# Scan layer of a four-layer stack: gate, SiLU, softplus steps and one spread of B moved within a task

## The reference

```python
xr = x @ in_w.T
u, res = (xr[..., :d_in], xr[..., d_in:])
...
u = _silu(jnp.transpose(uc + conv_b[None, :, None], (0, 2, 1)))
A = -jnp.exp(Alog)
xdbl = u @ xproj_w.T
delta = jax.nn.softplus(xdbl[..., :dt_rank] @ dt_w.T + dt_b)
Bm = xdbl[..., dt_rank:dt_rank + D_STATE]
Cm = xdbl[..., dt_rank + D_STATE:]
dA = jnp.exp(jnp.einsum('bld,dn->bldn', delta, A))
dBu = jnp.einsum('bld,bln,bld->bldn', delta, Bm, u)
...
    h = dA_t * h + dBu_t
    return (h, jnp.einsum('bdn,bn->bd', h, C_t))
...
y = jnp.moveaxis(ys, 0, 1) + u * D
y = y * _silu(res)
return y @ out_w.T
```

## Time and profile before

| | |
|---|---|
| median of 3 runs | 21318.11 us (21314.53 to 21318.33) |
| profiled execution, its own time | 21309.68 us |
| its span | 21307.9 us |
| VectorE (DVE) busy | 18447.0 us, 87% |
| GpSimd (POOL) busy | 17170.0 us, 81% |
| TensorE (PE) busy | 13655.5 us, 64% |
| ScalarE (ACT) busy | 11409.1 us, 54% |
| scan layer | from about 2250 to 18000 us |

### The profile page before, as it was taken

How to read it: one execution, slowest core, us unless ns; L and a number is a source line. 1 busy time by engine, 2 the same in 40 slices (tenths; PEclk the granted TensorE clock), 3 DMA queues, 4 the chain that set the end, 5 groups by cost and what they waited for, 6 DMA issues and landing times. The chain is left out here.

```text
span 21307.9 us, 183765 instructions
## 1 busy us (share of the span) xinstructions
PE 13655.5 (64%) x47074; PEld 4924.9 (23%) x47074; DVE 18447.0 (87%) x11898; ACT 11409.1 (54%) x12716; POOL 17170.0 (81%) x7352
## 2 busy tenths in 40 slices
PE   4875665665565565565565565565565668888885
PEld 2331111111111111111111111111111124444444
DVE  5778888888888888888888888888888878888886
ACT  1115555555555555555555555555555546666663
POOL 3768888888888888888888888888888868888881
PEclk8887777777777777777777777777777779999997
DMA  3225445545545545545445545545545521111113
GB/s 118 93 88 124 122 117 125 122 119 125 122 116 125 122 119 125 122 117 125 123 119 124 123 117 124 123 119 124 123 117 124 123 69 29 30 30 30 31 29 131
DMA packets 615483, 2240.63 MB, mean 105 GB/s; under 512 B 74881, under 2 KB 92147, under 8 KB 591091
## 3 DMA queue, kind: packets, MB, share of 16 engines
q1 hardware_dynamic: 610146, 2232.63, 41.6%
q10 hardware_dynamic: 5265, 7.14, 0.1%
HBM read 990.77 MB, written 174.96 MB: 55 GB/s over the span
## 5 line engine op out<-in xcount | busy, mean ns | idle before, releaser
L1357 POOL TENSOR_TENSOR h<-h,c_bc 128x1024 f32<-128x1024 f32 x4096 | 9593.6, 2356 | 1393.6 <-DVE h L1309 1393.1
L1309 DVE TENSOR_TENSOR_SCAN h<-da,state,px 128x1024 f32<-128x1024 f32 x3328 | 7810.8, 2347 | 444.7 <-DVE px L1303 165.2
L1174 ACT ACTIVATE da<-d_bc,a_neg 128x1024 f32<-128x1024 f32 x3328 | 3784.1, 1144 | 4012.1 <-DVE h L1309 3990.2
L1303 DVE TENSOR_TENSOR px<-px,du_bc 128x1024 f32<-128x1024 f32 x3328 | 4098.4, 1231 | 442.0 <-PE px L1002 221.2
L1016 PE MATMUL py<-h,ysel 128*32 128x512 f32 x16384 | 2784.6, 814 | 1039.1 <-POOL h L1357 1039.1
L1002 PE MATMUL px<-cf,bsel 32*128 32x512 f32 x4096 | 1536.0, 834 | 2677.6 <-DVE h L1309 2677.6
L1946 POOL TENSOR_TENSOR acc<-acc,ta 128x1024 f32<-128x1024 f32 (+1 forms) x1040 | 2425.1, 2339 | 500.7 <-DVE acc L1846 373.6
L1309 DVE TENSOR_TENSOR_SCAN h<-px,state,xs 128x1024 f32<-128x1024 f32 x768 | 1776.7, 2341 | 856.4 <-ACT px L1174 856.4
L1846 DVE SCALAR_TENSOR_TENSOR p_c<-zb,w_dw,p_c 128x1024 f32<-128x1024 f32 (+1 forms) x1560 | 1986.3, 1273 | 43.7 <-PE p_c L1618 11.4
L1349 POOL TENSOR_TENSOR xs<-du_bc,b_bc 128x1024 f32<-128x1024 f32 x768 | 1803.4, 2348 | 0.0
L1324 POOL TENSOR_TENSOR delta<-delta,sp 128x1024 f32<-128x1024 f32 x256 | 601.5, 2350 | 1166.8 <-ACT sp L1126 1166.8
(11 more groups left out here) (222 smaller groups left out, 20608.7 us busy)
## 6 DMA issues: line engine op xcount, KB each, us to landing
d_bc<-delta SPq DMA_DIRECT2D x1024, 512.0 KB, 8.1
du_bc<-du SPq DMA_DIRECT2D x1024, 512.0 KB, 8.6
c_bc<-c_rows_dram SPq DMA_DIRECT2D x1024, 512.0 KB, 5.0
b_bc<-c_rows_dram SPq DMA_DIRECT2D x256, 512.0 KB, 8.0
hx<-x_dram SPq DMA_DIRECT2D x252, 256.5 KB, 5.9
st_x<-in_x_dram SPq DMA_DIRECT2D x32, 1024.0 KB, 4.8
ax<-in_x_dram SPq DMA_DIRECT2D x64, 512.0 KB, 3.4
xr<-x_dram SPq DMA_DIRECT2D x64, 512.0 KB, 5.8
```

Of the source, the lines that this page charges most:

```text
L1174: nc.scalar.activation(out[:, :], d_bc[:, n % J, :], ACT.Exp, scale=a_neg[t.l][:, n:n + 1]).then_inc(da_done, 1)
L1303: nc.vector.tensor_tensor(out=x[:, :], in0=b[:, :], in1=du_bc[:, j, :], op=ALU.mult).then_inc(m1_done, 1)
L1309: nc.vector.tensor_tensor_scan(h[:, n % 8, PAD:T + PAD], a[:, :], x[:, :], state[:, 2 * t.l + t.b, n:n + 1], ALU.mult, ALU.add).then_inc(s ...
L1357: nc.gpsimd.tensor_tensor(out=h[:, n % 8, 0:T], in0=h[:, n % 8, PAD:T + PAD], in1=c_bc[q % 2][:, :], op=ALU.mult).then_inc(m2_done, 1)
```

## The change

Four edits, all in the scan layer:

- GATE_AT goes from 3 to 2 (VectorE gates the task before behind scan 2), DL_AT from 7 to 6 and DU_AT from 8 to 7 (GpSimd's delta and du).
- In `front_silu` the wait for the gate of two tasks before (yg_done) goes from ahead of the first half of u to ahead of the first half of sr; ahead of u stands a wait for du_done of the same task, the last reader of that u buffer on GpSimd.
- TensorE: `front_bc` in front of `skip`, `front_dt` in front of `add_y(t, 0)`, `spread_b(t, 3)` in front of `add_y(t, 1)`.
- ScalarE: `front_bc` ahead of decay 11, `front_abs` ahead of decay 12, `front_exp` ahead of decay 8, `front_ln` right behind decay 8.

```diff
@@ -793,8 +793,8 @@
         gnorm = GroupNorm(nc, ctx, "l1", bn1, pair, pm)
         block = ctx.enter_context(nc.Block())
 
-        GATE_AT, STATS_AT = 3, 6
-        OUT_AT, DL_AT, DU_AT, ZN_AT = 0, 7, 8, 13
+        GATE_AT, STATS_AT = 2, 6
+        OUT_AT, DL_AT, DU_AT, ZN_AT = 0, 6, 7, 13
         POOL_X_AT = {0: 0, 2: 1, 3: 2}
 
         DECAYS = (0, 1, 2, 3, 4, 5, 6, 7, 11, 12, 8, 13, 9, 10, 14, 15)
@@ -1037,17 +1037,16 @@
                 spread_b(t, 1)
                 if after:
                     front_res(after)
+                    front_bc(after)
                 skip(t)
                 if after:
-                    front_bc(after)
+                    front_dt(after)
                 add_y(t, 0)
-                if after:
-                    front_dt(after)
                 if before:
                     back_z(before, t, after)
                 spread_b(t, 2)
+                spread_b(t, 3)
                 add_y(t, 1)
-                spread_b(t, 3)
                 if before:
                     back_var(before)
                 add_y(t, 2)
@@ -1087,7 +1086,7 @@
 
             def front_silu(t):
                 if t.from_(2):
-                    act.wait_ge(yg_done, t.nth() - 2)
+                    act.wait_ge(du_done, t.nth() - 2)
                 for i in range(2):
                     cut = slice(i * HALF, (i + 1) * HALF)
                     act.wait_ge(u_ps, t.nth(i, 2))
@@ -1095,6 +1094,8 @@
                 for i in range(2):
                     cut = slice(i * HALF, (i + 1) * HALF)
                     act.wait_ge(res_ps, t.nth(i, 2))
+                    if i == 0 and t.from_(2):
+                        act.wait_ge(yg_done, t.nth() - 2)
                     nc.scalar.activation(sr[t.par][:, cut], pm[:, cut], ACT.Silu).then_inc(sr_done, 1)
                 act.preload_act_table_set("natural_log_exp_and_others")
 
@@ -1193,20 +1194,20 @@
                 if after:
                     front_silu(after)
                 decay(t, 7)
+                if after:
+                    front_bc(after)
                 decay(t, 11)
                 keep_state(t, 0)
                 if after:
-                    front_bc(after)
+                    front_abs(after)
                 decay(t, 12)
                 if after:
-                    front_abs(after)
+                    front_exp(after)
                 decay(t, 8)
                 if after:
-                    front_exp(after)
+                    front_ln(after)
                 decay(t, 13)
                 decay(t, 9)
-                if after:
-                    front_ln(after)
                 decay(t, 10)
                 decay(t, 14)
                 if before:
```

## The result

| | before | after |
|---|---|---|
| median of the runs (4 each) | 21318.22 us | 20589.9 us (20572.38 to 20602.02) |
| profiled execution, its own time | 21309.68 us | 20572.38 us |
| its span | 21307.9 us | 20570.6 us |
| ratio after / before | | 0.9658, 95% interval 0.9641 to 0.9675 |

The change saves 728 us, 3.4%; 861 were predicted. The forecast was 20455 in a range of 20250 to 20720, so the time lies inside, and about a sixth of the gain is missing. The loss lies inside the task: the scan layer (first to last scan) became 720.7 us shorter, of 737.3 in the span. It runs from 1623 to 17343 us before and from 1621 to 16620 after; the 2250 to 18000 given for it ahead of the prediction was wrong, and windows from 2200 on leave out the first nine or ten of its 256 tasks.

What follows compares the result with a forecast made beforehand. VectorE's work plus 4.19 us a task of waits was taken as the bound; 4.19 less 0.8 left gives 3.4 over 254 tasks, 861 us, so 20457 from the median, predicted as 20455, range 20250 to 20720.

Steps and rivals of the forecast that it cites:

- The bound of a task: Scan layer: VectorE's own work plus 4.19 us a task of waits, 3.34 for ScalarE's decays and 0.85 for TensorE's B.
- costs nothing while that lead lasts: VectorE's gate behind scan 2: free while the last y sum it needs ends ahead of it, a lead of 1.0 us.
- This part alone is worth 0 to 0.1 us: ScalarE: freeing the first half of SiLU from the gate gains 0 to 0.1 us, as decay 6 waits for scan 2 too.
- Load to the end of SiLU, 6.46: ScalarE: first table load to the end of the gate's SiLU takes 6.46 us, so that SiLU ends at 10054.9.
- rival 3: ScalarE: a table switch costs more right behind an activation, at most another 1.28 us; 325 less gain, 20780 us; chance 0.03.
- B/C, skip, delta in a row: 7.08: TensorE: the three products take 3.17 + 1.93 + 1.98 = 7.08 us, so Abs can start 4.9 us sooner.
- little changes: TensorE: if B/C becomes as slow as skip was, the skip behind it becomes quicker and little changes.
- Scan 9, 0.7: VectorE: decay 9 ends near 70.3, scan 8 near 69.6, so scan 9 still waits 0.7 us, as before.
- bounds 0 and 0.4, taken 0, since TensorE then has more work in a row: Scan 12's wait for the y sum behind B's spread: 0 us at the high clock level, 0.4 at the low; taken 0.
- 0.7 of slack stays: SP's queue: late spreads of du and their multiply both move forward by about 3.5 us, leaving 0.7 us of slack.
- rival 2: Transfers: spreads of du land after 10.2 instead of 9.1 us, costing some 1 us a task; 20710 us; chance 0.13.
- costs nothing by itself: GpSimd: delta's sum one step sooner, ahead of product 7, costs nothing; product 11 ends 3.5 us sooner.

Runs made afterwards that it cites:

- gate alone: Kernel before with only GATE_AT changed from 3 to 2, so the gate stands behind scan 2; 20444.57 us, ratio 0.9594.
- e3: Changed kernel with ScalarE's old order of softplus steps and decays (decay 8 behind Relu, Ln behind decay 9); 20584.16 us, ratio 0.9658.
- e8: Changed kernel with ScalarE's old order and also DL_AT 7, DU_AT 8 as before; 20331.06 us, ratio 0.9537.
- e11: Kernel of e8 with the y sum of group 1 ahead of both spreads of B on TensorE; 20403.37 us, ratio 0.9575.
- SiLU alone: Kernel before with only the first half of SiLU freed of the gate's wait, gate still behind scan 3; 20443.15 us, ratio 0.9593.
- gate and spread: Kernel before with GATE_AT 2 and the spread of B for group 3 ahead of the second y sum; 20438.19 us, ratio 0.9588.

## Why the prediction came out as it did

The mechanism of the gain held, and the time lies in the range. Of the prediction's own signs of being wrong one showed, the wait of scan 12 for the y sum (0.49 a task), and another barely, multiplies that wait for a spread of du (4.2 us in all). The table load starts 1.20 behind scan 2 as forecast, the task lasts 58.6 instead of 58.0, Abs starts 15.3 behind the gate's start instead of 14.8, and the wait for decays is 1.03 where under 1 was given, with 0.42 of it at scan 8 instead of nearly all at scan 9. Step by step:

- **The bound of a task** (4.19 of waits, from the chain behind the gate and from multiply 12) is shown: moving the gate alone takes the decays' wait from 823.9 to 14.5 and 863 us from the kernel. That this is the 861 predicted for the whole change is chance: the gate alone takes the decays' 3.34 and leaves multiply 12's 0.82, while the forecast left 0.8 at the decays and took multiply 12's wait.
- **Gate behind scan 2, "costs nothing while that lead lasts"**: right; in 247 tasks the gate waits once for the y sum, 6.2 us in the last task (5.9 before).
- **"This part alone is worth 0 to 0.1 us"** holds for the SiLU edit only beside the moved gate, which is how it was meant (put back in the change, 1.5 us of difference). By itself it is worth the whole 870 us. My expectation for the change without the moved gate forgot that, and missed by 870 or more. Two edits that remove the same wait must be priced as one.
- **Load to the end of SiLU, 6.46**: 7.61 - 1.20 = 6.41 on the mean. The two table loads cost their 1.28 each and nothing else: decay 6 starts at 10070.98, the load at 10072.14 and u at 10073.44, with no idle time in any row. The Trainium skill, ScalarE: Activation LUTs, section What ACT_TABLE_LOAD costs, adds a drain of about 1.38 us to a switch; with the load right behind an activation this trace has no room for one, so rival 3 is out, and the measurement decides against the page's figure here.
- **"B/C, skip, delta in a row: 7.08"** was mis-sized: from the end of sr to Abs it is 7.57 on the mean (15.18 - 7.61; less than the sum of 7.71, since each product starts a little before the row of the one ahead of it ends). B/C now runs at the low level (3.58 against 1.94), and the skip product got back only part of that (2.25 against 3.19). The prediction named this exchange and booked it as "little changes"; it was 0.5. Decay 8 starts 19.18 behind scan 2, where 66.1 - 47.28 = 18.8 was predicted, so scan 8 comes 0.49 late instead of 0.1 (scan 7 to scan 8 takes 2.75 on the mean, 2.26 where nothing waits; the profile's idle time, counted from the end of scan 7, is 0.42).
- **Scan 9, 0.7**: 2.95 from scan 8 on the mean, 2.24 at the least: 0.7 (0.62 by idle time; with scan 8's 0.42 the 1.03 of the groups). This is the price of the new softplus order. The step that is missing here is one that I didn't take: I priced the order as it stood and never asked what the old one would have given beside the earlier gate. It leaves next to nothing (4.1 us in all in e3, 13.6 in e8).
- **The y sum, "bounds 0 and 0.4, taken 0, since TensorE then has more work in a row"**: 0.49. The reason was wrong: in the task shown both spreads start behind 6.49 of idle time and run at the 1.2 GHz level, and most of the sum with them. The bound itself was sound: part of the 0.49 is the short gap that scan 12 has anyway behind its multiply, and net of it scan 12 starts 4.13 behind scan 11, where it is 3.83 in e11 without that wait, so 0.3.
- **Du's spreads, "0.7 of slack stays"**: it stayed (4.2 us in all), but only since the decays' waits stand between. Late spreads of du, rival 2's result, are real, though not by its way: the old ScalarE order shows them at once, 303.5, with landings as short as ever and a later issue. What I had as "costs nothing by itself" (delta one step sooner) costs 253 us there.

In the sum: 1.52 left instead of 0.8 is 0.72 x 254 = 183 us less gain, and the short gaps that went with scan 12's wait give 0.17 x 254 = 43 back: 861 - 183 + 43 = 721, for 720.7 measured in the layer.

What stays open: the four kernels gate alone, SiLU alone, gate and spread, and y sum first have the same task length, 58.03 on the mean over tasks 20 to 235, though their waits stand in different places and two of them differ in TensorE's order; their times differ (20403 for y sum first, 20438 to 20445 for the others) only by their first and last tasks and by what lies outside the layer. The traces show one thing more of them. Over tasks 40 to 215 every turn of four tasks lasts 232.0 to 232.2 us, and the granted clock changes at the same places of each turn: taken every half microsecond from a turn's start, two neighbouring turns have the same level in over 99% of the places on the mean. The kernel before is as regular (245.8), the kernel after is not (233.5 to 235.2, 83%). So the length of a task and the pattern of the clock seem tied together in these kernels. Then their total time doesn't tell what one edit is worth, and that the spread of B is worth nothing, or the y sum first 72 us too much, holds for these kernels as they stand and not for the edit in itself. How the two are tied wasn't tried.

## What to carry to other kernels

Read the chain behind a late instruction back to its first wait, and take that wait away alone before anything else: here one number gave 863 us, and with four more edits on top 728 of them were left. An edit that shows no effect in a bundle may be hidden by another one (ScalarE's order and DL_AT are each worth 250 us, but only where the other is right), so test pairs of edits as a table of four. An instruction put earlier in an in-order queue delays all behind it by its own wait: delta waited 3.59 us for the Ln ahead of a product that a transfer was waiting for.

## What the runs showed of the hardware

- TensorE's level decides the same product's time nearly twofold within one task, again and again: B/C 1.93 or 3.67, a spread 1.13 or 2.07, the y sum 1.93 or 3.64; the stretches read were granted 1.00 around the short ones and 0.50 to 0.53 around the long ones. Moving a 1 us product elsewhere changed which products ran at which level (gate and spread: skip 3.40 to 3.78, B/C 1.93 to 2.47), so a duration read before the change was no safe price for the same product in its new place. The Trainium skill, TensorE: Matmul & The Clock Gate, section HAM oscillation — how this bites in real kernels, describes such a swing for a kernel that waits for a transfer in every round of its loop; this one, whose TensorE waits for other engines, has it too, at a mean granted clock of 0.772.
- Tasks that lasted 61.32 to 61.67 each before (scan 3 to scan 3, tasks 20 to 235) range over 58.1 to 60.1 in the kernel after. Decay 8 starts 21.54 to 21.66 behind scan 2 before and 18.47 to 20.25 after, and scan 8 then starts 2.26 to 3.90 behind scan 7. In this chain skip takes 1.98 to 3.78 from task to task, B/C 3.27 to 3.68 and delta always 1.88.
